# PSUM banks given out singly, one transfer for each rotated half, and another table of priorities in a two-layer transformer kernel

## The reference

```python
def reference(x, ...):
    x = x + L0_attn_a(_layernorm(x))   # "band": 16 heads of 64, rope, window of 128 back
    x = x + L0_ffn(_layernorm(x))      # "ffn0": gated, hidden 384, integer weights
    x = x + L0_attn_b(_layernorm(x))   # "causal": 16 heads of 8, rope, causal mask
    x = x + L0_ffn(_layernorm(x))
    x = x + L1_attn_a(_layernorm(x))   # "chunk": 16 heads of 8, chunks of 64 tokens, rope
    x = x + L1_ffn(_layernorm(x))      # "ffn1": gated, hidden 352, fp4 quantised inputs and weights
    x = x + L1_attn_b(_layernorm(x))   # "lowrank": 16 heads of 8, no mask
    x = x + L1_ffn(_layernorm(x))
    return x

def _L0_attn_a_ref(hidden_states, Wq, bq, Wk, bk, Wv, bv, Wo, bo):   # band
    q = _apply_rope(proj(Wq, bq)); k = _apply_rope(proj(Wk, bk)); v = proj(Wv, bv)
    ...
    band = (kj >= qi) & (kj <= qi + W)
    scores = jnp.where(valid[None, None], scores, -1e30)
    attn = jax.nn.softmax(scores, axis=-1)
    ctx = jnp.einsum('bhnqk,bhnkd->bhnqd', attn, vcat)
    return merged @ Wo.T + bo
```

## Time and profile before

| | |
|---|---|
| median of 3 runs | 2120.56 us (2117.95 to 2127.51) |
| the profiled execution | 2124.22 us, of which the span of its instructions 2122.0 |
| PE busy | 1731.3 us |
| DVE, POOL, ACT busy | 1345.2, 972.0, 788.8 us |
| mean granted clock of PE | 0.90 of full |
| DMA | 122.00 MB, of which 512 transfers of 64 KB from `quad_r` to `band_r` |
| idle time ahead of ACT's `probs` (exp), waiting for PE | 335.3 us |

### The profile page before, as it was taken

How to read it: one execution, slowest core, us unless ns; L and a number is a source line. 1 busy time by engine, 2 the same in 40 slices (tenths; PEclk the granted TensorE clock), 3 DMA queues, 4 the chain that set the end, 5 groups by cost and what they waited for, 6 DMA issues and landing times.

```text
span 2122.0 us, 50629 instructions
## 1 busy us (share of the span) xinstructions
PE 1731.3 (82%) x20493; PEld 1184.8 (56%) x20493; DVE 1345.2 (63%) x2752; ACT 788.8 (37%) x1238; POOL 972.0 (46%) x1362
## 2 busy tenths in 40 slices
PE   3689888989888997889999987777777788888874
PEld 3355555555655556655555556676665555555543
DVE  4555665555555435666565546777777678888883
ACT  1233333333333332234444443333333344444451
POOL 3333333223233214434343345788885555555543
PEclk8799999999999999999999999987877788888897
DMA  5222111211111210023333233333342223323210
GB/s 172 53 47 51 46 45 44 49 41 41 41 41 43 50 30 16 16 60 76 76 73 79 61 76 69 83 79 77 77 89 49 46 48 66 66 66 65 56 31 8
DMA packets 191894, 122.00 MB, mean 57 GB/s; under 512 B 17569, under 2 KB 173986, under 8 KB 191538
## 3 DMA queue, kind: packets, MB, share of 16 engines
q1 hardware_dynamic: 191442, 118.23, 24.2%
q0 software_dynamic: 224, 0.54, 0.1%
HBM read 45.31 MB, written 39.85 MB: 40 GB/s over the span
## 4 chain that ended last, share of the span: by engine, by line
PE 55%; DVE 23%; ACT 9%; issue 6%; POOL 4%; SPq 1%; DMA 0%; DVEq 0%; POOLq 0%; ACTq 0%
PE slots L1342 39%; PE ctx_ps L1342 11%; DVE nmx L1214 8%; DVE rope_part L1256 5%; ACT probs L1100 3%; PE slots L1630 2%; DVE rope_part L1179 2%; DVE ctxT L1318 1%; ACT ctxT L1019 1%; SPq L875 1%; DVE band_r L1180 1%; ACT band_va L1019 1%; ACT band_rb L1019 1%; PE slots L1383 1%; DVE rope_part L1180 1%
## 5 line engine op out<-in xcount | busy, mean ns | idle before, releaser
L1214 DVE TENSOR_REDUCE nmx<-slots 128x8 f32<-128x1024 f32 (+2 forms) x352 | 411.9, 1216 | 171.6 <-PE slots L1342 170.8
L1100 ACT ACTIVATE probs<-slots 128x1024 f32<-128x1024 f32 (+1 forms) x416 | 356.8, 892 | 338.8 <-PE slots L1342 335.3
L1342 PE MATMUL slots<-band_r 64*64 64x64 bf16 (+4 forms) x5120 | 398.9, 268 | 62.7 <-DVE nmx L1214 38.1
L1342 PEld LDWEIGHTS slots<-band_r 64*128 64x128 bf16 (+2 forms) x5120 | 199.8, 125 | 235.1 <-issue 130.4
L997 POOL TENSOR_TENSOR quad_r<-rope_part 128x512 f32<-128x512 f32 x128 | 162.5, 1279 | 285.3 <-DVE rope_part L1256 156.2
L1342 PE MATMUL slots<-mask,ident_bf 128*128 128x256 bf16 (+1 forms) x896 | 224.0, 333 | 65.4 <-DVEq L1263 20.4
L1342 PE MATMUL ctx_ps<-probs,band_va 64*32 64x64 f32 (+4 forms) x5120 | 261.0, 318 | 13.3 <-issue 8.9
L1256 DVE SCALAR_TENSOR_TENSOR rope_part<-slots,bias_qk,rope_band 128x256 f32<-128x256 f32 x512 | 206.4, 476 | 101.5 <-POOL quad_r L997 74.3
L1342 PE MATMUL slots<-nmT,pick 64*128 64x256 bf16 (+2 forms) x2560 | 225.7, 252 | 0.0
L1342 PEld LDWEIGHTS ctx_ps<-probs,band_va 128*32 128x32 f32 (+2 forms) x5120 | 145.6, 119 | 97.1 <-issue 52.0
L911 POOL TENSOR_TENSOR var_eps<-mean_var,eps 128x2 f32<-128x2 f32 x128 | 29.2, 228 | 268.2 <-DVE mean_var L1142 267.6
(11 more groups left out here) (179 smaller groups left out, 3048.8 us busy)
## 6 DMA issues: line engine op xcount, KB each, us to landing
band_r<-scratch SPq DMA_DIRECT2D x192, 192.0 KB, 4.3
band_r<-quad_r SPq DMA_DIRECT2D x512, 64.0 KB, 2.0
scratch<-parts SPq DMA_DIRECT2D x96, 192.0 KB
scratch<-parts SPq DMA_DIRECT2D x96, 128.0 KB
scratch<-parts SPq DMA_DIRECT2D x96, 64.0 KB
x<-in_x SPq DMA_DIRECT2D x16, 128.0 KB, 4.5
out<-x SPq DMA_DIRECT2D x16, 128.0 KB, 1.8
band_r<-in_band_qk SPq DMA_DIRECT2D x1, 1024.0 KB, 6.3
```

Source lines behind the costliest of these rows:

```text
L1100: nc.scalar.activation(probs[:, g % 2, step[2], :, 0:width], slot(u, step).rearrange("p (a n) -> p a n", a=2)[:, :, 0:width], ACT.Exp, sca ...
L1214: nc.vector.tensor_reduce(dst, src, axis=AX.X, op=ALU.max, negate=True).then_inc(free_sem(u, step), 1)
L1342: return nc.tensor.matmul(o, lhsT, rhs, start=start, stop=stop, skip_group_check=shared)
```

## The change

1. **PSUM.** The planner keeps what holds each of the six banks (`held`, `BANKS`). A fill for which `narrow` is true takes one bank: of those free by its start, the one whose partner in the pair is freed last. A wide fill takes an aligned pair of banks, the pair whose later bank is freed first. There are 3 + 6 semaphores: one for each pair, one for each bank; `take` waits for the release of every fill that last held one of its banks, one or two waits. `slot` gives 512 or 1024 columns. The low-rank `qk` writes its two parts side by side in 512 columns.
2. **Rotated halves.** The 128 partitions of `quad_r` hold the same four heads in another order, and in `band_r` first and second halves alternate (first on even, second on odd partitions of a head), so that one transfer of 256 KB from 128 partitions to every second of 128 partitions, two chunks, takes a half: 2 a quad, 128 in all. Rope table, weights and biases are permuted on the host. The planner's cost of SP's step is 0.65 where it was 2.55.
3. **The table.** All 82 values of `LEAD` differ, and `PER_UNIT` is 0.0236 where it was 0.0286.
4. **DVE.** `stats` waits, but for the first time, until its last aggregation is done (`var_ready`).

The diff, cut to its core (the other engines' tables change in the same way):

```diff
-        "rot": [("dve", 1.56), ("pool", 1.29), ("sp", 2.55)],
+        "rot": [("dve", 1.56), ("pool", 1.29), ("sp", 0.65)],
...
 LEAD = {
     "pe": {
-        "tail": {"band": 0.579, "causal": 31.687, "chunk": 21.49, "lowrank": -1.167},
-        "finish": {"causal": 0.382, "chunk": 0.222, "lowrank": -0.145, "end": -0.665},
-        "forward": {"causal": 8.832, "chunk": -0.145, "lowrank": 18.653, "end": -1.158},
-        "operands": {"band": 20.005, "causal": 1.174, "chunk": 24.896, "lowrank": 76.144},
-        "maxima": {"band": 0.021, "causal": 0.721, "chunk": 4.511, "lowrank": -1.567},
-        "back": {"band": 0.08, "causal": -0.17, "chunk": -0.646, "lowrank": -1.576},
+        "tail": {"band": 28.06, "causal": 10.671, "chunk": 15.417, "lowrank": 30.583},
+        "finish": {"causal": -2.81, "chunk": -0.371, "lowrank": -0.139, "end": 0.212},
+        "forward": {"causal": 44.628, "chunk": 81.464, "lowrank": -0.096, "end": 0.708},
+        "operands": {"band": 17.571, "causal": 47.467, "chunk": 2.26, "lowrank": 20.934},
+        "maxima": {"band": 14.636, "causal": 0.943, "chunk": 1.101, "lowrank": -0.619},
+        "back": {"band": 17.432, "causal": -0.185, "chunk": -0.589, "lowrank": -0.625},
...
-PER_UNIT = 0.0286
+PER_UNIT = 0.0236
...
+def narrow(kind, step):
+
+    name = step[0]
+    if name == "v":
+        return kind != "band"
+    if name == "qk":
+        return kind == "lowrank"
+    if name == "ffn":
+        return step[1] == 2 and AHEAD[kind] == "ffn0"
+    return name in ("xT", "down", "nm", "den", "rden", "ctx", "ctxT", "out")
...
-    held = [[] for _ in range(SLOTS)]
+    held, counts = [None] * BANKS, [0] * (SLOTS + BANKS)
...
-        known = [(done[of[-1]] if of else 0.0, s) for s, of in enumerate(held) if not of or of[-1] in done]
-        slot_at, slot = min(known) if known else (None, None)
+        at = [0.0 if fill is None else done.get(released_by(*fill), UNKNOWN) for fill in held]
+        wide_at = min(max(pair) for pair in zip(at[0::2], at[1::2]))
+        narrow_at = min(at)
...
-            slots[u, step] = slot, len(held[slot])
-            held[slot].append(released_by(u, step))
+            if narrow(UNITS[u][0], step):
+                free_now = [i for i in range(BANKS) if at[i] < UNKNOWN and at[i] + WAKE["pe"] <= start]
+                first = max(free_now, key=lambda i: (at[i ^ 1], -i))
+                taken, sem = [first], SLOTS + first
+            else:
+                first = min(range(0, BANKS, 2), key=lambda i: (max(at[i], at[i + 1]), i))
+                taken, sem = [first, first + 1], first // 2
+            waits = {held[i]: None for i in taken if held[i] is not None}
+            slots[u, step] = first, sem, counts[sem], tuple((slots[fill][1], slots[fill][2] + 1) for fill in waits)
...
-                        for i in range(4):
-                            to = 64 * (i % 2) + 32 * second
-                            sp.dma_start(band_r[to:to + 32, b % RING, 2 * m + i // 2],
-                                         quad_r[32 * i:32 * i + 32, quad % 2, second]).then_inc(band_moved[quad % 2], 16)
+                        sp.dma_start(band_r[int(second)::2, b % RING, 2 * m:2 * m + 2],
+                                     quad_r[:, quad % 2, int(second)]).then_inc(band_moved[quad % 2], 16)
...
                 def stats(b):
 
+                    if taken[0]:
+                        dve.wait_ge(var_ready, 2 * taken[0])
+                    taken[0] += 1
...
                 def take(u, step):
 
-                    at, filled = SLOT[u, step]
-                    if filled:
-                        pe.wait_ge(slot_free[at], filled)
-                    return slots[:, at, :]
+                    for i, filled in SLOT[u, step][3]:
+                        pe.wait_ge(slot_free[i], filled)
+                    return slot(u, step)
...
-    quads = feat.reshape(QUADS, 4, 2, BIG_D // 2).transpose(0, 2, 1, 3).reshape(QUADS, 2, P)
+    quads = feat.reshape(QUADS, 2, 2, 2, BIG_D // 2).transpose(0, 3, 2, 4, 1).reshape(QUADS, 2, P)
```

More of the change, by code:

```diff
@@ L54 @@
 SLOTS = 3
+BANKS = 2 * SLOTS
+UNKNOWN = 1e18
 WEIGHTS_AT = 5
@@ L304 @@
[L304 to L307, removed]
+        "tail": {"band": 65.567, "causal": -7.984, "chunk": -2.521, "lowrank": -5.797},
+        "finish": {"lowrank": 47.748, "end": -44.447},
+        "forward": {"causal": 59.115, "chunk": 66.518, "lowrank": 0.993, "end": 31.241},
@@ L308 @@
+        "operands": {"band": 26.057, "causal": -35.306, "chunk": -14.747, "lowrank": -10.355},
+        "back": {"band": 15.28, "causal": -10.615, "chunk": -13.161, "lowrank": 28.755},
     },
     "dve": {
[L310 to L313, removed]
@@ L314 @@
-        "maxima": {"band": -2.962, "causal": -51.183, "chunk": 30.291, "lowrank": 36.608},
+        "tail": {"band": 8.717, "causal": 1.575, "chunk": 17.427, "lowrank": 2.368},
+        "finish": {"causal": -58.568, "chunk": 27.715, "lowrank": 1.925, "end": -3.63},
+        "forward": {"causal": 58.806, "chunk": 45.807, "lowrank": 2.118, "end": -3.955},
+        "operands": {"band": -15.813, "causal": 1.918, "chunk": 2.246, "lowrank": 25.243},
+        "maxima": {"band": 23.077, "causal": 40.048, "chunk": -18.384, "lowrank": 34.566},
@@ L315 @@
     },
     "pool": {
-        "tail": {"band": -42.083, "causal": 40.938, "chunk": 0.066, "lowrank": 6.629},
-        "finish": {"causal": -27.454, "chunk": -49.756, "lowrank": 9.302, "end": 76.825},
-        "forward": {"causal": 1.399, "chunk": -20.38, "lowrank": 19.311, "end": 52.875},
-        "operands": {"band": 6.442, "causal": -8.743, "chunk": 50.085, "lowrank": 11.974},
-        "maxima": {"band": 8.799, "causal": 24.457, "chunk": -6.764, "lowrank": 62.179},
+        "tail": {"band": 35.515, "causal": -13.678, "chunk": -36.907, "lowrank": -57.155},
@@ L322 @@
+        "finish": {"causal": 42.104, "chunk": -15.067, "lowrank": -38.746, "end": 45.221},
+        "forward": {"causal": 31.463, "chunk": 66.879, "lowrank": 7.554, "end": 33.736},
+        "operands": {"band": -13.854, "causal": 4.59, "chunk": 4.876, "lowrank": 5.084},
+        "maxima": {"band": 16.581, "causal": -11.062, "chunk": -13.332, "lowrank": 66.941},
     },
 }
-PER_UNIT = 0.0286
+PER_UNIT = 0.0236
 def settles(step, eng):
     return LANDS[step[0]] if eng == "sp" else SETTLE[eng]
+def narrow(kind, step):
[7 more added lines that the diff above has]
+    return name in ("xT", "down", "nm", "den", "rden", "ctx", "ctxT", "out")
@@ L414, in make_plan @@
                 if eng == "pe" and step[0] in FRONT_FILLS + BACK_FILLS:
-                    if slot is None or any(w not in done for w in opens[u, step]):
+                    slot_at = narrow_at if narrow(UNITS[u][0], step) else wide_at
+                    if slot_at == UNKNOWN or any(w not in done for w in opens[u, step]):
                         continue
@@ L575, in build @@
         slots = ps("slots", [P, SLOTS, 1024])
+        slots_flat = slots[:].rearrange("p s n -> p (s n)")
         ctx_ps = ps("ctx_ps", [P, TILES, 512])
@@ L591, in build @@
         back_full = sem("back_full")
-        slot_free = [sem(f"slot_free{i}") for i in range(SLOTS)]
+        slot_free = [sem(f"slot_free{i}") for i in range(SLOTS + BANKS)]
         xh_ready = sem("xh_ready")
@@ L831, in slot @@
         def slot(u, step):
-            return slots[:, SLOT[u, step][0], :]
+            first = 512 * SLOT[u, step][0]
+            return slots_flat[:, first:first + (512 if narrow(UNITS[u][0], step) else 1024)]
         def free_sem(u, step):
-            return slot_free[SLOT[u, step][0]]
+            return slot_free[SLOT[u, step][1]]
         def released(eng, u, step):
-            eng.wait_ge(slot_free[SLOT[u, step][0]], SLOT[u, step][1] + 1)
+            eng.wait_ge(slot_free[SLOT[u, step][1]], SLOT[u, step][2] + 1)
         def walk(eng, front_half, back_half):
```

25 lines of the change are left out of this document (14 added, 11 removed).

## The result

The changed kernel takes 2157.7 us, the median of 4 runs (2149.1 to 2161.8), beside 2122.2 for the kernel before on the same chip: a ratio of 1.016 with an interval of 1.012 to 1.020. It is slower, where 2065 us was forecast with a chance of 0.77 for faster. Its profiled execution took 2154.2 us, 2151.9 of it the span.

A forecast was written before the change was run, and what follows sets the result against it. TensorE (PE), busy 82% of the span, was taken to set the time, through its idle time and clock. Terms -7 - 9 - 15 - 20 - 5 = -56 us from 2124.2 gave 2068.2, as a median 2065 us; range 2005 to 2118.

The forecast's parts named there:

- The start: First sequence: one transfer a half brings the first score fill to about 53.5 us from 60.73; 7 us (bounds 3, 8).
- Releases of qk slots: Band, after the start: faster transfers release `qk` slots earlier, a third of PE's waits on DVEq L1263; 9 us (bounds 0, 28).
- not under 30: Sign of the transfer part: POOL's wait for the rotated-half transfers, 129.0 us before, falls under 30 us.
- rival 1: Whole kernel: transfer hidden but for the start, freed banks expose data waits, table keeps what was there; 2111 us, chance 0.13.
- Banks: PSUM: narrow fills in one bank cut waits behind foreign drains, two thirds of 23.5 us; 15 us (bounds 0, 31).
- named as the sign: Waits of `nm` and the L1409 transposes behind foreign drains fall under half.
- The table: Order on every engine: PE idle filled mostly by score fills put between `S` and `V` fills; 20 us gain.
- rival 3: Chunk and lowrank: wide fills wait for long-lived narrow fills' drains, 2.4 us a sequence, +77; 2142 us, chance 0.09.
- The clock: Chunk and lowrank: less PE idle time gives back some of the granted clock; 5 us (bounds 0, 44).
- over 0.82: Sign: granted clock in chunk over 0.82, where it was 0.79, and over 0.90 in lowrank.
- Rival 4: Rotated-half transfer: alternate destination rows slow it, landing takes 5 us or more, part 1's gain lost; 2081 us, chance 0.07.

The follow-up runs named there:

- old order with both parts: Kernel before with its order of every engine frozen, plus one transfer a half and PSUM given out by banks: 2105.7 us, ratio 0.9913.
- orders a to c: Changed kernel with step orders from new priority searches using durations from traces: a 2039.3 us, b (another start) 2061.0, c (a searched on) 1998.0.
- order c: Changed kernel with the order from a search continued from order a, using durations and wake-up times from more traces: 1998.0 us, ratio 0.9425.
- old table under new rules: Changed kernel's banks and transfer with the old table and PER_UNIT, the planner making another order from it: 2237.4 us, ratio 1.0552.

## Why the prediction was wrong, point by point

**The start (7 us, bounds 3 and 8): right, a little small.** With the transfer alone the first score fill came 7.7 us earlier, some 3 more followed by 4% of the work, and the median gained 11. The transfer took 2.4 us, inside the bounds of 2.0 and 3.8, and near the 2.6 that the Trainium skill's fit gave in the prediction.

**Releases of qk slots (9 us): nothing.** The wait behind DVEq is 25.4 us with one transfer as with four. It is DVE's own pace, as the prediction said of most of it; the third that I still took was not there. POOL's wait halved (58.0 us with the transfer alone, not under 30), and behind the start nothing on PE hung on it: rival 1 was right on this point.

**Banks (15 us): mis-sized.** 7 to 9 us alone, 5 on top of the transfer. The rows that I added up as curable, `nm` and the ffn transposes behind foreign drains, went from 30.7 to 28.3 us in the old order. In the changed kernel they did fall, as I had named as the sign (11.4 to 0.7 and 13.2 to 4.2): through the order, and while the kernel became slower. A wait that vanishes from its row is not time gained.

**The table (20 us): the step that failed.** I had bounded it below by the idle time it could fill and took a small share of that, with the other end left to rival 3. It costs 52 us. Against the old order with both parts the new one is 20 us ahead at 44% of the work and level again at 64%; the piece from there to 76% takes 334 us instead of 279:

```profile
1293.00:1572.00 279.00, 214.22 (x5230) 188.90 (x5230) 207.03 (x493) 102.50 (x191) 226.92 (x316) 0.80 0.34 79
```

and its largest issue row there, where the changed kernel has 21.1:

```profile
PE ctx_ps L1418 <- issue: 1.7, 2, 1.4
```

Of the 55 us, 21.4 are PE being busy longer and 33.6 idle; of the idle, issue grew from 2.3 to 32.0. Two moves of one step gave back 24. The error in reasoning: I took a table found anew as a reason to expect a gain and asked only how much idle time it could fill. Had I walked the two frozen orders with the costs of `work`, the walk would have said 1.4 us, and that there is no ground for 20. It would hardly have said a loss: with the durations that are written into orders a to c, without stops, the walks end at 2080.7 and 2085.8, a loss of 5 us; and if PE's durations are taken from the trace of before alone, the only one there was then, at 2121 and 2119. The size of the loss, 52 us, no walk gives.

**The clock (-5 us): the sum came, by another way.** Over the whole run PE is busy 1725.8 us for the same matmuls, 5.5 less than before and 8.7 less than in the old order with both parts (1734.5), and the mean granted clock of the profiled runs is 0.914, for 0.901 and 0.895. But "less idle time gives some of it back" was not the reason, since PE stands idle 35 us more. The clock fell where the time was lost, to 0.78, where the old order has 0.80, order c 0.88 and the forecast over 0.82, and PE is busy 21 us longer there than in the old order; in all the rest it is busy 30 us less, with 0.90 of full over lowrank, as forecast there. That the term is met is luck. Between orders the clock can weigh more than this term: PE's busy time is 1764.5 us for the old table under new rules and 1665.2 in order c.

**Rival 3 (2142 us, chance 0.09)** had the sign and about the size, but not the mechanism, so it is no hit. That wide fills wait for the drains of `down` and `ctx` doesn't show: in the lost piece the waits that end on those drains, other than for data, are under 1 us, and with the old order the same banks gain 7 us. And where PE stands for over 1 us ahead of a chunk `qk`, the bank that comes free last is that of its own `xT`, whose data it needs anyway. Rival 4 is out by the landing of 2.4 us. **The range** (up to 2118) was too narrow because the table's poor end was taken as 0 inside the forecast, though the text said that no row prices an order.

Not settled: the 28 to 30 us that remain between the changed kernel with `qk` moved and the old order, in the same piece of work, and why the stops are long in one order and short in the next with the same run. I have not tried a kernel with fewer instructions in `V`.

## What to carry to other kernels

A schedule found by a planner is worth what its costs are worth: freeze the old order and run it with the new rules before believing in the new one, and walk both with durations from a trace. In the table above two walks by the planner's own costs that differ by 2.4% still have the wrong sign; by the traces' durations pairs up to 0.8% apart do, and all that are 3% and more apart came true. Search long and test several orders on the chip: four searched orders lay between 1998 and 2061 us, with walks within 24 us of one another. And compare two orders at equal work, not at equal time; the 55 us were lost in 12% of the work. Before a filler is called work inside a wait, see in its own row that the wait isn't ahead of it.

## What the runs showed of the hardware that I had not expected

PE can run short of instructions. In runs of 64-column matmuls it stopped inside a step for 0.4 to 4 us, each of the 196 stops at a multiple of 256 of its instructions (plus 121 or 122, by the count above), and went on 2.2 to 3.2 us after a 16 KB packet on the instruction queue had started; 37 us of the changed kernel, 5.5 us in the old order with both parts. In the other stages, with longer matmuls, it cost next to nothing.

Thrown-away matmuls that PE had to do on top, ahead of `qk`, raised the granted clock of the stretch (0.78 to 0.85) and shortened the other work by 19 us, about what they cost, 20.6 us.

From the end of a PE step (its end is modelled) to the start of the waiting ACT or DVE pass 0.04 us in about half of the pairs and up to 0.11 in the others; from the end of ACT or DVE to PE's matmul 0.055 or 0.145 us. Both values of each stand in the traces of before and of the changed kernel.
